# Softmax attention in a macaron block: row maxima from 64-row products, row sums packed on 32 rows and their inverse copied back by DMA, the output product in float16 halves

## The reference

```python
HEADS, DIM_HEAD, EPS = 16, 64, 1e-10
def safe_softmax(s):
    m = jnp.max(s, axis=-1, keepdims=True)
    e = jnp.exp(s - m)
    return e / (jnp.sum(e, axis=-1, keepdims=True) + EPS)
q, k, v = split_heads(x @ Wq.T), split_heads(x @ Wk.T), split_heads(x @ Wv.T)
sim = jnp.einsum('bhid,bhjd->bhij', q, k) * DIM_HEAD ** -0.5
attn = safe_softmax(sim)
out = jnp.einsum('bhij,bhjd->bhid', attn, v)
return out.transpose(0, 2, 1, 3).reshape(B, N, INNER) @ Wo.T + bo
```

## Time and profile before

| | us |
|---|---|
| median of 3 runs | 2223.76 |
| the profiled execution | 2225.31 |
| its span, first to last instruction | 2223.6 |
| PE busy in the span | 1599.6 (72%) |
| DVE busy | 1569.2 (71%) |
| POOL busy | 1028.3 (46%) |
| ACT busy | 912.8 (41%) |

### The profile page before, as it was taken

The page is one execution under the profiler, slowest core; times in us unless marked ns, Lnnn a source line. Parts: engine busy times, 40 slices in busy tenths (PEclk is TensorE's granted clock), DMA queues, the critical chain, the costliest instruction groups (busy, mean ns, idle before and its releaser), DMA issues. The chain is left out here.

```text
span 2223.6 us, 29789 instructions
## 1 busy us (share of the span) xinstructions
PE 1599.6 (72%) x9139; PEld 934.4 (42%) x9139; DVE 1569.2 (71%) x3212; ACT 912.8 (41%) x2102; POOL 1028.3 (46%) x1332
## 2 busy tenths in 40 slices
PE   0546389999999999999965563158658888830686
PEld 0334134444444444444423343135437767730453
DVE  5887778878788888877878886336467777752563
ACT  0112255555555555555522221035336676610452
POOL 0111245555555555555532224635435555546353
PEclk9889599999999999999987895579879999955898
DMA  6000022222222222222200000122300000001224
GB/s 186 0 0 1 23 63 58 58 58 58 63 59 61 60 59 58 58 58 59 62 9 1 0 0 24 56 77 80 104 16 1 1 1 1 1 32 62 75 81 145
DMA packets 126010, 104.05 MB, mean 47 GB/s; under 512 B 19680, under 2 KB 120480, under 8 KB 125856
## 3 DMA queue, kind: packets, MB, share of 16 engines
q1 hardware_dynamic: 111616, 77.75, 13.6%
q0 software_dynamic: 8704, 18.89, 2.5%
q10 hardware_dynamic: 5536, 5.52, 0.8%
HBM read 29.32 MB, written 22.30 MB: 23 GB/s over the span
## 5 line engine op out<-in xcount | busy, mean ns | idle before, releaser
L770 ACT ACTIVATE at_pT<-at_turned 128x512 f32<-128x512 f32 x512 | 305.6, 597 | 290.3 <-PE at_turned L837 271.2
L669 DVE TENSOR_REDUCE at_nmax<-at_score 128x1 f32<-128x512 f32 x512 | 337.1, 680 | 69.8 <-PE at_score L814 66.8
L648 POOL TENSOR_TENSOR m_rows<-at_pT 128x512 f32<-128x512 f32 x128 | 162.5, 1269 | 375.1 <-ACT at_pT L770 375.1
L691 DVE RECIPROCAL m_rows<-m_rows 128x512 f32<-128x512 f32 x64 | 214.6, 3353 | 37.7 <-ACT m_rows L776 37.7
L875 PE MATMUL at_pv<-at_pT,at_v 128*64 128x512 f32 x1024 | 230.6, 592 | 0.0
L814 PE MATMUL at_score<-at_kh,at_both 128*128 128x512 f16 x512 | 196.7, 385 | 22.6 <-DVE at_nmax L669 17.0
L1056 POOL DMA_INDIRECT by_token<-m_ysb,m_dest x144 | 138.2, 960 | 144.7 <-DVE m_ysb L1136 109.5
L836 PE MATMUL at_turned<-at_both,at_kh 128*128 128x512 f16 x512 | 194.9, 381 | 0.4 <-ACT at_pT L770 0.3
L837 PE MATMUL at_turned<-at_both,at_kl 128*128 128x512 f16 x512 | 194.8, 380 | 0.0
L656 POOL TENSOR_TENSOR m_rows<-m_rows,at_pT 128x512 f32<-128x512 f32 x128 | 162.8, 1272 | 10.6 <-ACT at_pT L770 0.7
L652 POOL TENSOR_TENSOR m_rows<-m_rows,at_pT 128x512 f32<-128x512 f32 x128 | 162.7, 1271 | 10.4 <-ACT at_pT L770 0.5
(11 more groups left out here) (309 smaller groups left out, 3685.0 us busy)
## 6 DMA issues: line engine op xcount, KB each, us to landing
at_both<-at_part_q SPq DMA_DIRECT2D x128, 128.0 KB, 2.4
at_kh<-at_part_k SPq DMA_DIRECT2D x256, 64.0 KB, 2.0
m_xin<-by_expert SPq DMA_DIRECT2D x144, 72.0 KB
at_both<-at_part_q SPq DMA_DIRECT2D x128, 64.0 KB, 2.1
at_kl<-at_part_k SPq DMA_DIRECT2D x128, 64.0 KB
m_rows<-by_token SPq DMA_DIRECT2D x32, 256.0 KB, 4.8
by_token<-m_ysb,m_dest POOLq DMA_INDIRECT x144
m_x<-in_x SPq DMA_DIRECT2D x8, 256.0 KB, 4.7
```

Of the source, the lines that this page charges most:

```text
L648: nc.gpsimd.tensor_tensor(acc, pT[g % 2][:, head, 0, :], pT[g % 2][:, head, 1, :], ALU.add).then_inc(chain, 1)
L669: nc.vector.tensor_reduce(nmax[head][:, qt:qt + 1], score[use % 2][:], AX.X, ALU.max, negate=True)\
L691: nc.vector.reciprocal(rinv, total).then_inc(rinv_done, 1)
L770: nc.scalar.activation(pT[g % 2][:, head, kt, :], turned[i % 2][:], ACT.Exp).then_inc(exp_done, 1)
```

## The change

Four edits, all in `attn_stage`.

1. Maxima. `scores(g, qt)` now multiplies only the float16 heads of q and k (`head_of`), straight from where ACT writes them: the two heads of a pair lie on rows 0 to 63 and 64 to 127, and their two products go to the two score banks. Both banks must be read before the next pair of products (`s_read` of all earlier ones). The maxima of both heads lie in one tile of 8 columns, are transposed once (`max_turned`, into a part of the bank `sums`) and copied by one DMA.
2. Sums. The ones are 32 columns wide. `add_up` writes four quarters of 32 rows, each for one half of the queries of one head, into 128 x 256 of `sums`; ACT and DVE work on 256 columns instead of 512. `spread` on SP copies each quarter of `packed` (32 rows x 256) twice, to the rows and columns of `rinv` where `normalise` needs it: eight DMAs a pair, behind `max_row` and ahead of the next pair's `q_rows`. `normalise` waits for all eight (`rinv_in`).
3. Output product. ACT writes the float16 head of `oT` (`o_head`), DVE the rest (`o_rest`), and `output` makes twelve float16 products of 128 columns with the float16 halves of 64 x `Wo` (`wo16`, made once at the start of the stage) instead of four float32 ones; `add_x` scales by 1/64. `normalise` of pair g-2, `o_head`, `o_rest` and `output` stand in period g.
4. Order. PE does v's projection of pair g at the period's end between the products of `values`, the transposed scores come before the scores, and all loops are written in the new order.

Cut to its core:

```diff
-        ones = mem["spare"][:, 0:DH]
+        ones = s.sb("ones", [P, QUAD])
+        o16 = mem["spare"].bitcast(F16).rearrange("p (a q) -> p a q", a=2)
+        max_bank = sums[0:UPP, HALF:HALF + P]
...
+                def spread(g):
+                    sp.wait_ge(packed_done, g + 1)
+                    if g:
+                        sp.wait_ge(o_done, g)
+                    for head in range(2):
+                        for half in range(2):
+                            first = (2 * head + half) * QUAD
+                            for to in (head * DH, head * DH + QUAD):
+                                sp.dma_start(rinv[to:to + QUAD, half * HALF:(half + 1) * HALF], packed[first:first + QUAD, :])\
+                                  .then_inc(rinv_in, 16)
+
+                sp.wait_ge(set_up, RING + 2)
                 for g in PERIODS:
-                    if live(g):
-                        max_row(g, 1)
                     if live(g + 2):
                         if g + 2 >= RING:
                             sp.wait_ge(t_done, 8 * (g + 3 - RING))
...
+                        q_rows(g + 2)
+                        k_rows(g + 2)
                     if live(g + 1):
...
+                        max_row(g + 1)
+                    if live(g - 1):
+                        spread(g - 1)
...
+                def invert(g):
                     dve.wait_ge(total_done, g + 1)
-                    nc.vector.reciprocal(rinv, total).then_inc(rinv_done, 1)
+                    if g:
+                        dve.wait_ge(rinv_in, 16 * R_DMAS * g)
+                    nc.vector.reciprocal(packed, total).then_inc(packed_done, 1)
 
                 def normalise(g):
-
                     dve.wait_ge(pv_done, g + 1)
-                    dve.wait_ge(rinv_done, g + 1)
-                    if g >= 2:
-                        dve.wait_ge(out_done, g - 1)
-                    nc.vector.tensor_tensor(oT[g % 2][:], pv[:], rinv, ALU.mult).then_inc(o_done, 1)
+                    dve.wait_ge(rinv_in, 16 * R_DMAS * (g + 1))
+                    if g:
+                        dve.wait_ge(o_low, g)
+                        dve.wait_ge(o_high, g)
+                    nc.vector.tensor_tensor(oT[:], pv[:], rinv, ALU.mult).then_inc(o_done, 1)
+
+                def o_rest(g):
+                    dve.wait_ge(o_high, g + 1)
+                    nc.vector.tensor_tensor(o16[:, 1, :], oT[:], o16[:, 0, :], ALU.subtract).then_inc(o_low, 1)
...
+                def scores(g, qt):
+                    if qt == 0:
+                        pe.wait_ge(hi_done, 2 * g + 2)
+                    if g or qt:
+                        pe.wait_ge(s_read, 8 * g + 2 * qt)
+                    for head in range(2):
+                        rows = halves[head]
+                        nc.tensor.matmul(score[head][:], head_of[0][g % 2][rows, qt * P:(qt + 1) * P], head_of[1][g % 2][rows, :],
+                                         start=True, stop=True).then_inc(s_done, 1)
+
+                def max_turned(g):
+                    pe.wait_ge(s_read, 8 * (g + 1))
...
+                    nc.tensor.transpose(max_bank, nmax[:], mem["ident"][:]).then_inc(m_done, 1)
...
+                def add_up(g):
                     pe.wait_ge(added, 2 * (g + 1))
...
                     for head in range(2):
-                        last = nc.tensor.matmul(sums[halves[head], :], ones[:], psum[g % 2][:, head, :], start=True, stop=True)
+                        for half in range(2):
+                            first = (2 * head + half) * QUAD
+                            last = nc.tensor.matmul(sums[first:first + QUAD, 0:HALF], ones[:],
+                                                    psum[g % 2][:, head, half * HALF:(half + 1) * HALF], start=True, stop=True)
                     last.then_inc(sums_done, 1)
...
                     for t in range(TPB):
                         tile = slice(t * P, (t + 1) * P)
-                        last = nc.tensor.matmul(out[:, tile], oT[g % 2][:, tile], mem["woT"][:, pair, :],
-                                                start=(pair == 0 and t == 0), stop=(pair == PAIRS - 1), skip_group_check=True)
+                        for i, (o_part, w_part) in enumerate(XY):
+                            last = nc.tensor.matmul(out[:, tile], o16[:, o_part, tile], wo16[:, w_part, pair, :],
+                                                    start=(pair == 0 and t == 0 and i == 0), stop=(pair == PAIRS - 1 and i == 2),
+                                                    skip_group_check=True)
                     last.then_inc(out_done, 1)
 
-                pe.wait_ge(set_up, RING + 3)
+                pe.wait_ge(set_up, RING + 2)
                 for g in PERIODS:
                     for i in range(UPP):
-                        if live(g + 1):
-                            scores(g + 1, i)
                         if live(g):
                             scores_turned(g, i)
-                        if i == 1 and live(g):
-                            max_turned(g, 1)
-                        if i == 2 and live(g + 2):
+                        if i % 2 == 0 and live(g + 1):
+                            scores(g + 1, i // 2)
+                        if i == 1 and live(g + 2):
                             project(g + 2, 0)
...
+                        if i == 6 and live(g - 2):
+                            output(g - 2)
+                        if i == 5 and live(g + 2):
+                            project(g + 2, 1)
+                    if live(g - 1):
+                        add_up(g - 1)
+                        values(g - 1, 0)
+                    if live(g + 1):
+                        max_turned(g + 1)
+                    if live(g - 1):
+                        values(g - 1, 1)
+                    if live(g):
+                        project(g, 2)
+                    if live(g - 1):
+                        values(g - 1, 2)
+                        values(g - 1, 3)
```

More of the change, by code:

```diff
@@ new lines, in q_rows, with k_rows @@
+                    sp.wait_ge(lo_done, 2 * g + 1)
+                    for head in range(2):
+                        sp.dma_start(both[k][DH:P, 0, head, :], rest_of[0][halves[head], :]).then_inc(q_in[k], 16)
+                def k_rows(g):
+                    k = g % RING
+                    sp.wait_ge(hi_done, 2 * g + 2)
+                    for head in range(2):
+                        for half in halves:
+                            sp.dma_start(kh[k][half, head, :], head_of[1][g % 2][halves[head], :]).then_inc(k_in[k], 16)
+                    sp.wait_ge(lo_done, 2 * g + 2)
+                    for head in range(2):
+                        sp.dma_start(kl[k][0:DH, head, :], rest_of[1][halves[head], :]).then_inc(k_in[k], 16)
@@ L720, in _ @@
                         neg_max(g + 1, 0)
+                    if live(g - 2):
+                        normalise(g - 2)
+                    if live(g + 1):
                         neg_max(g + 1, 1)
-                    if live(g):
-                        max_row(g, 1)
+                    if live(g + 2):
+                        low(g + 2, 0)
+                    if live(g - 2):
+                        o_rest(g - 2)
                     if live(g + 1):
@@ L854, in project @@
                             last = nc.tensor.matmul(proj[:], w[:, w_part, cols], x(x_part, 0, SEQ), start=(i == 0), stop=(i == 2))
+                        last.then_inc(qk_done, 1)
                     else:
```

256 lines of the change are left out of this document (109 added, 147 removed).

## The result

| | before | after |
|---|---|---|
| median of the comparison's runs | 2224.69 us (2223.67 to 2231.09, 4 runs) | 2489.06 us (2484.18 to 2492.69, 4 runs) |
| profiled execution, span | 2225.3, 2223.6 us | 2484.18, 2482.5 us |
| mean granted clock over the span | 0.882 | 0.842 |
| mean period of the attention stage | 13.38 us | 17.38 us |

A forecast was written before the change was run, and what follows sets the result against it. PE set the pace before; afterwards a loop through DVE, PE and SP's eight copies would: 4.16 + 3.38 + 1.95 + 6.48 plus 0.2 makes 16.2 us a period. 175 + 4 + 45 = +224 us gives 2448; range 2365 to 2525.

The forecast's parts named there:

- handovers, loss by the low clock: Attention loop: some 0.2 us for five handovers between engines, plus 0.7 us a period for PE's low clock.
- The copies on SP: SP's queue: eight DMAs issued in series, 4.48 us, plus 2.0 landing, 6.48 us between inverse and `normalise`.
- The clock: PE idles about 3 us each period, then runs at half clock; 0.7 us a period (0 to 1.5), 45 us.
- Signs: Attention-stage trace: L699 released by a copy DMA, PE busy below 80%, clock 0.85 to 0.97, periods 16 to 17.2 us.
- Rival 1: Attention stage: the chain of copies holds but the clock stays up; 2403 us, chance 27%.
- Rival 2: SP's copies are hidden if issued within 0.19 us each, PE sets the pace with 0.4 less; 2198 us, chance 4%.
- Rival 3: PE's tile switches dominate at 0.2 us instead of 0.1, period 17.85 us; 2509 us, chance 5%.
- PE's own work: PE's savings on scores, sums, output and one transposition, less 0.8 us for tile switches: 0.4 us a period saved.
- rivals 2 and 4: Rival 4, beside rival 2: issues at about 0.25 us pay back what PE saves; 2224 us, chance 2%.
- The sums: PE: eight sum instructions of half the columns take 0.65 us, between 0.46 (four side by side) and 0.91.
- The output product's 0.66: PE: twelve float16 products take about 0.66 us instead of 0.86 to 1.05, saving 0.2 us.
- the scores' 0.86: PE: 64-row score products of two heads run side by side, four times 0.21 us, saving 0.86 us.

The follow-up runs named there:

- filler kernel: Changed kernel plus 36 products on 128 columns, result unread, ahead of the third pair of scores in PE's gap; ratio 1.0857, period 16.30 us.
- the fastest kernel: Changed kernel with `normalise` later, maxima's row sent by ACT, scores on 128 rows, value quarter 1 directly ahead of 2 and 3; ratio 0.9822, period 12.61 us.

## Why the prediction was right, and which term was off

The mechanism and its place were as forecast. Of the loop's terms (all start to start, changed kernel, the period shown above; in the last term but one 0.06 is handover, as the filler kernel shows, and 0.84 low clock):

| term | predicted | measured |
|---|---|---|
| DVE from `normalise` to the end of the third pair of reductions | 4.16 | 608.61 to 612.89: 4.28 |
| PE from the last scores to DVE's copy | 3.38 | 613.79 to 617.20: 3.41 |
| DVE, copy and reciprocal | 1.95 | 617.20 to 619.14: 1.94 |
| SP, inverse ready to `normalise` | 6.48 | 601.96 to 608.61: 6.65 |
| handovers, loss by the low clock | 0.2 + 0.7 | 612.89 to 613.79: 0.90 |
| period | 16.9 | 17.18 shown, 17.38 in the mean |

- *The copies on SP.* Right. Issue steps of 0.66 against 0.64, landing 1.9 against 2.0, together 6.48 forecast and 6.42 in the median period; the dose of eight, six and four copies confirms it. The issue time doesn't follow the size: 32 rows cost as much as 64 and 128.
- *The clock.* Right that it falls, too small. Predicted 0.7 a period; the filler gives back 17.38 - 16.30 = 1.08. With the clock up the loop is 16.30, where the prediction had 16.2. This term is the one that was mis-sized: the prediction had 1.7 - 0.5 = 1.2 of a slow stretch fall on the loop, but took 0.7, since "it won't come in every period". It does come in nearly every period: in 58 of 59 the last scores start more than 0.2 us behind the reductions that they wait for, 0.93 in the mean, in the filler kernel in 2 of 58. The slack in front of them was put about right: with the clock up PE idles 0.39 us there (607.09), against 0.5. And some of the slow stretch falls behind the last scores, where PE's way to the copy takes 3.77 in the mean, against 3.45 with the filler.
- *What the sum was off by.* The spans differ by 258.9, the sum had 224: 34.9 too few. A period got 4.00 longer instead of 3.44: 0.38 of this is the clock, 0.1 the rest of the loop, 0.08 the period before, 13.38 in the mean where the prediction multiplied 13.46 by 64. Over 63 periods that makes 35. Outside them the spans differ by 6.7, where the prediction had one period more (3.4) and 4. The other 6 of the 41 us: the median of the changed kernel lies 5 above its profiled execution, and 1.5 had been taken off the sum.
- *Signs.* Two of the prediction's signs were missed narrowly: PE is busy 82% of the stretch 400 to 1000 us, not below 80, and the mean period of 17.38 is above 17.2. The copies are not named as the releaser of L699 in 61 of 64 periods.
- *Rival 1*, clock stays up, 2403 us: fell, the clock of the stretch 400 to 1000 us was 0.89. The filler kernel is what it would have been: 1.0857 x 2224.69 = 2415.
- *Rival 2*, copies hidden: its break-even of 0.19 us an issue was never near. The Trainium skill (DMA: Bandwidth & Descriptors, Issuing engines are not separate DMA queues) calls the time to initiate a DMA usually small relative to the DMA; here it is 0.66 against 1.9, and eight in a row are the loop's largest term. The rival's second half, a PE that then sets the pace with 0.4 less, holds only in another order: with no copies at all the period is 13.76, 0.38 above before, since PE's waits for two banks grew by as much. With `normalise` later it is 13.09 and 13.06, 0.3 below before.
- *Rival 3*, tile switches: 0.10 us each way, as taken, not 0.2. They did not dominate, but they eat all that the 64-row products save.
- *PE's own work.* The four savings in the prediction's list add up to 1.52, less 0.8 for the switches 0.72, and not the 0.4 that it goes on with; only rivals 2 and 4 rest on the 0.4. Measured it is 0.34 (12.69 against 13.03 a period, `normalise` later). The sums were put at 0.65 and take 0.57: four tiles of 32 columns run side by side. The output product's 0.66 holds (0.68). Of the scores' 0.86 their own switches leave 0.14 a period (3 x 0.01 + 0.11, as worked out above). Not in this sum was that each pair needs both banks free, which shows as waits only where no copies hold the kernel up.

## What to carry over

A chain of small transfers costs its issue times in series plus one landing; from 32 to 128 rows the issue time was the same here. Ask not how long that is but when its result is first wanted: here the same eight copies cost nothing, but for the stage's last three pairs, once their consumer stood behind two more pairs of reductions and the rest of q, some 3 us of DVE's work (the output product moved with it), and most of 4 us a period where it stood early. Price a wait on TensorE twice, once as time and once as the slow clock after it, and count the second in every period unless a row shows otherwise. And count what a denser tile shape saves only after the changes into and out of it.

## What was not expected of the hardware

- Idle TensorE time costs more than itself, here more than was forecast. After 3.05 us without a product the granted clock was 0.53 for the next 2.95 us, where the dense parts of the same period show 1.00; 36 useless products in that gap brought the ratio from 1.118 down to 1.0857.
- A change of tile shape took 0.10 us both ways for 64-row pairs; before, only the way out of the value products was visible.
- DVE's subtraction with a float16 result (`o_rest`) took 0.68 us and more for the same shape: its median over the stage is 682 ns in the changed kernel, 921 with `normalise` later, 886 in the fastest kernel and 1447 in that with the output product half a period later. The traces show what it waits for: an instruction that GpSimd (POOL) has already begun. These are POOL's rows around the 1.13 us that DVE's L707 took from 611.59 to 612.72:

```profile
610.91 1.26 POOL L651 TENSOR_TENSOR m_rows<-at_pT 128x512 f32<-128x512 f32 x1
612.25 1.60 POOL L655 TENSOR_TENSOR m_rows<-m_rows,at_pT 128x512 f32<-128x512 f32 x1
```

POOL's L651 ends at 612.17, DVE's L707 0.55 later. The same holds for `o_rest` in twelve kernels between 330 and 1090 us: wherever a POOL instruction ran on for more than 0.15 us behind its start, it ended 0.54 to 0.56 us after that instruction (460 times), and wherever none did it took 0.68 to 0.71 (177 times). POOL's next instruction is held up in turn, 1.60 us here instead of 1.27. DVE's `normalise` keeps its 0.68 to 0.69 in every kernel. So what stands on POOL beside an instruction of DVE can decide what it costs; why `o_rest` is held up and `normalise` is not, no run tells.
